# Dense weights built eight groups ahead instead of five, dense products from tile 15 instead of 22, and a reordered hand-over into the second sum of a fused graph kernel

## The reference

```
agg_l  = segment_sum((h @ W_l.T)[src] * norm, dst)          # 3 rounds
h      = elu(agg_l + b_l) + h
x1     = layernorm(x + concat(h0..h3) @ lin_w.T + lin_b)
W_r    = sum_b w_comp[r, b] * bases[b]                       # 8 relations, 4 bases
agg_r  = segment_sum(x1[src] * edge_weight, type * N + dst)
out    = layernorm(x1 + sum_r agg_r[r] @ W_r)
```

## Time and profile before

| | us |
|---|---|
| median of 3 runs | 1145.95 |
| lowest, highest | 1143.07, 1146.01 |
| the profiled execution | 1150.11 |
| its span in the trace | 1148.3 |
| from the first row of chunk 0 on PE to the end of the span | 579 |

### The profile page before, as it was taken

The page is one execution under the profiler, slowest core; times in us unless marked ns, Lnnn a source line. Parts: engine busy times, 40 slices in busy tenths (PEclk is TensorE's granted clock), DMA queues, the critical chain, the costliest instruction groups (busy, mean ns, idle before and its releaser), DMA issues.

```text
span 1148.3 us, 23479 instructions
## 1 busy us (share of the span) xinstructions
PE 1043.0 (91%) x9505; PEld 691.3 (60%) x9508; DVE 817.7 (71%) x1702; ACT 445.0 (39%) x1027; POOL 509.9 (44%) x542
## 2 busy tenths in 40 slices
PE   1678889889999999995489999999999999999997
PEld 1566556555644564465366666676666666666665
DVE  4689899887546556887566776876876776776753
ACT  1588889887300040025233332332332332332320
POOL 5043000000067400000377777776776766766761
PEclk9777899889999999997589999999999999999999
DMA  6163000000111010100422222222212212212210
GB/s 162 43 186 90 1 1 1 1 1 1 56 22 27 9 56 1 48 9 15 130 55 54 59 54 59 58 52 54 59 49 56 58 50 54 59 49 54 58 49 24
DMA packets 48801, 55.34 MB, mean 48 GB/s; under 512 B 15543, under 2 KB 39129, under 8 KB 48182
## 3 DMA queue, kind: packets, MB, share of 16 engines
q0 software_dynamic: 16240, 31.95, 11.2%
q1 hardware_dynamic: 32454, 21.87, 6.6%
HBM read 42.10 MB, written 8.49 MB: 44 GB/s over the span
## 4 chain that ended last, share of the span: by engine, by line
PE 72%; DVE 13%; issue 5%; SPq 3%; DMA 2%; POOL 2%; ACT 2%; DVEq 1%; ACTq 0%
PE ps L1679 21%; PE ps L1532 20%; PE ps L1658 15%; PE ps L1673 10%; DVE arena L1108 8%; PE ps L1521 2%; SPq L681 2%; POOL arena L838 2%; PE ps L1686 1%; PE ps L1692 1%; PE ps L1479 1%; SPq L738 1%; DMA dinv_col<-dinv_scratch 1%; DVE arena L1262 1%; PE ps L1509 1%
## 5 line engine op out<-in xcount | busy, mean ns | idle before, releaser
L838 POOL DMA_INDIRECT arena<-x_scratch,arena x437 | 412.9, 945 | 195.2 <-issue 124.2
L1532 PE MATMUL ps<-arena,u 125*128 125x480 fp8e5 (+1 forms) x1575 | 363.0, 357 | 1.2 <-ACT arena L892 1.2
L973 ACT COPY arena<-ps 125x400 f32<-125x400 f32 x364 | 169.6, 524 | 390.0 <-PE ps L1673 367.5
L1679 PE MATMUL ps<-arena,u 125*128 125x448 f32 x650 | 296.0, 539 | 0.0
L1658 PE MATMUL ps<-hT,arena 128*128 128x192 f32 x874 | 226.5, 352 | 13.1 <-DMA arena<-x_scratch,arena 13.0
L1532 PEld LDWEIGHTS ps<-arena,u 125*128 125x128 bf16 x1575 | 153.5, 98 | 107.9 <-ACT arena L892 1.7
L1658 PEld LDWEIGHTS ps<-hT,arena 128*128 128x128 f32 x874 | 148.8, 192 | 97.1 <-issue 67.7
L1108 DVE TENSOR_TENSOR arena<-arena 128x2048 bf16<-128x2048 bf16 (+2 forms) x158 | 188.9, 1253 | 18.5 <-PE ps L1521 15.5
L1521 PE MATMUL ps<-arena 128*128 128x125 bf16 x1256 | 151.9, 236 | 32.4 <-DVE arena L1108 30.7
L1673 PEld LDWEIGHTS ps<-dinv_all,u 64*128 64x128 bf16 x4368 | 108.4, 96 | 107.4 <-issue 92.2
L1323 DVE TENSOR_TENSOR u<-ps,arena 128x512 bf16<-128x512 bf16 x182 | 76.5, 420 | 122.7 <-PE ps L1673 114.0
(11 more groups left out here) (187 smaller groups left out, 717.1 us busy)
## 6 DMA issues: line engine op xcount, KB each, us to landing
arena<-x_scratch,arena POOLq DMA_INDIRECT x437
arena<-hT SPq DMA_DIRECT2D x2, 1562.5 KB, 7.1
edge_scratch<-arena SPq DMA_DIRECT2D x5, 403.0 KB, 5.5
arena<-in_x_dram SPq DMA_DIRECT2D x1, 1562.5 KB
dinv_all<-dinv_scratch SPq DMA_DIRECT2D x1, 1562.5 KB, 8.5
h_scratch<-hT SPq DMA_DIRECT2D x1, 1562.5 KB, 6.9
first_term_scratch<-arena SPq DMA_DIRECT2D x1, 1562.5 KB
arena<-first_term_scratch SPq DMA_DIRECT2D x1, 1562.5 KB
```

The costliest lines, as they stand in the source:

```text
L838: nc.gpsimd.indirect_dma_start(out=gat[:, j, :], out_offset=None, in_=x1_d, in_offset=bass.IndirectOffsetOnAxis(ap=idxg[:, j:j + 1], axis= ...
L973: nc.scalar.copy(o, ps[0:BLK, octet_bank(k, w), 0:4 * ND].rearrange("p (i m) -> p m i", i=4)).then_inc(s_se, 1)
L1532: return T.matmul(ps[:, agg_bank(l, c), 0:CW[c]], u[0:BLK, s, k, :], region[:, s, 0:CW[c]], start=(first and s == 0 and k == 0), stop=(end ...
L1679: last = T.matmul(ps[:, 5, 0:NB * DN].rearrange("p (b n) -> p b n", b=NB), xb[0:BLK, s, :], sD[half][0:BLK].rearrange("p (b v) n -> p b v ...
```

## The change

- `QA` goes from 5 to 8: three more octets in the prologue, three fewer in chunk 12.
- `DJ` goes from 22 to 15: a full chunk does 18 of its own products and 7 of the previous chunk's, in place of 11 and 14. `DLEFT` goes from 14 to 7.
- In chunk 12 the products stand one per tile from tile 15, not two per tile from 22; the last chunk of 8 tiles gets 7 of them in place of 3, and its `finish_dense` and `finish` move from tile 5 to tile 7.
- The two refills are bound to the octet's number in its own group (`prepare`): they now stand ahead of the octets after tile 14 and after tile 30 of a chunk, and one in the prologue; before, after tile 4 and after tile 21.
- SP no longer waits for `s_var` ahead of the x1 stores; the load of the basis matrices is issued behind them.
- DVE's third coefficient part is made after the loop over the seven groups, not before it.

```diff
-    QA = 5
-    DJ = 22
+    QA = 8
+    DJ = 15
@@ sync
-            sp.wait_ge(s_var, NUB)
-            sp.dma_start(basesS[:, :, :], bases.rearrange("b i o -> i b o")).then_inc(s_bas, 16)
             for j in range(NUB):
                 ...
                 sp.wait_ge(s_x1, j + 1)
                 sp.dma_start(x1_d[...], xb[0:BLK, b0:b1, :]).then_inc(s_x1d, 16)
+            sp.dma_start(basesS[:, :, :], bases.rearrange("b i o -> i b o")).then_inc(s_bas, 16)
@@ vector
-            dve.wait_ge(s_cq, 4)
-            V.tensor_tensor(coefP[:, :, 2 * NB:3 * NB, :], coefT, coefP[:, :, NB:2 * NB, :], ALU.subtract).then_inc(s_cp, 1)
             for t in range(NUB + 1):
                 ...
+            dve.wait_ge(s_cq, 4)
+            V.tensor_tensor(coefP[:, :, 2 * NB:3 * NB, :], coefT, coefP[:, :, NB:2 * NB, :], ALU.subtract).then_inc(s_cp, 1)
             dve.wait_ge(s_back[0], 32)
@@ vector, second sum
+                def prepare(c, k):
+                    h, m = c + k // QD, k % QD
+                    if m == HQ and h + 1 < DH:
+                        refill(h + 1, 0, False)
+                    if m == 0 and h >= 1:
+                        refill(h, 1, False)
...
-                                if k == HQ and following == TPB:
-                                    refill(c + 1, 0, False)
-                                if k == QD:
-                                    refill(c + 1, 1, False)
+                                prepare(c, k)
                                 octet(c, k)
...
                 for k in range(QA):
+                    prepare(0, k)
                     octet(0, k)
@@ tensor, second sum
                         if j >= DJ:
-                            for s in ((j - DJ,) if following else (2 * (j - DJ), 2 * (j - DJ) + 1)):
-                                dense(s, half)
+                            dense(j - DJ, half)
...
                 for j in range(LTILES):
                     tile(C, j, LTILES)
-                    if 2 * (TPB - DJ) + j < NBLK:
-                        dense(2 * (TPB - DJ) + j, 0)
-                    if j == 2 * BT - 1:
+                    if j < DLEFT:
+                        dense(TPB - DJ + j, 0)
+                    if j == LTILES - 1:
                         finish_dense(DH - 1, 6)
                         pe.wait_ge(s_af, C)
                         pe.wait_ge(s_dv, DH - 1)
```

## The result

The changed kernel takes 1129.24 us (median of 4, 1125.61 to 1131.82) against 1145.89 (median of 4): over all runs a ratio of 0.9859, interval 0.9832 to 0.9885. The forecast was 1130.0.

A forecast was written before the change was run, and what follows sets the result against it. PE's work bounds the full chunks; before chunk 0, PE waits on the chain of x1, stores, gather, tile 0. Terms -9.9 + 0.5 - 10.8 + 4.3 = -15.9 us from median 1145.95 give 1130.0 us, range 1124 to 1138.

The forecast's parts named there:

- Loop over the groups earlier: Hand-over on DVE: without L1253 ahead of it, the loop starts and x1 is complete 5.4 us earlier.
- DVE's gap: Ahead of L1282: the 2.44 us of flag reading and branch may vanish under L1253; taken as 0.1 us.
- Prologue: Before chunk 0: octets start 1.86 us apart, the ninth at 559.4, so tile 0 can start at 560.5.
- rival 3: Hand-over does not move: the last store's landing holds the first gather; only chunks 12 and 13 gain, 1139.5; chance 0.08.
- Stores: SP at the hand-over: some 2.3 us to issue each, keeping up with the groups; first gather by 545.5, 14.5 us earlier.
- Chunk 0: First chunk after the prologue: ends at 599.4 against 609.3, gain 9.9 us, with 2.5 us charged for cold PE.
- Chunks 1 to 11: Full chunks: DVE may stall PE in tiles 7 to 14, without products; 0 to 1.1 us in all, taken 0.5.
- Chunk 12 and the last chunk: End of the second sum: chunk 12 saves 10.8 us of products and octets; L1692 in the last chunk costs 4.3.
- Sum: Whole kernel: the terms add to -15.9 us, giving 1130.0 us from the median 1145.95.
- The clock: PE in the prologue: all nine octets charged at granted clock 0.50; a rise to 1.00 would save up to 4 us.
- rival 2: The prologue warms: octet activity raises PE's clock, shortening the prologue; 1123.5 to 1127 us; chance 0.12.

The follow-up runs named there:

- e4: Kernel before with only DVE reordered: third coefficient part behind the loop over the groups; 1140.8 us, ratio 0.996.
- e1: Kernel before with the reordered hand-over alone (x1 stores without s_var wait, basis load behind them, third coefficient part behind the loop), QA 5, DJ 22; 1130.3 us, ratio 0.9872.
- e6: Changed kernel with the refill of the second half ahead of octet 16 of a chunk instead of octet 14; 1126.2 us, ratio 0.9832.
- e5: Changed kernel with extra matmuls of zeros that keep PE busy before and between the prologue octets; 1127.0 us, ratio 0.9845.
- e2: Changed kernel with the old hand-over put back (basis load ahead of the stores, third coefficient part ahead of the loop), QA 8, DJ 15; 1143.0 us, ratio 0.9982.
- e8: Changed kernel with DJ back at 22 and the last chunk as before, QA 8 and the new hand-over kept; 1125.9 us, ratio 0.9832.
- e7: Changed kernel with both the extra zero matmuls on PE and the later refill of the second half; 1127.3 us, ratio 0.984.
- e3: Kernel before with only SP reordered: x1 stores without the wait for s_var, basis load behind them; 1132.7 us, ratio 0.9892.
- e11: Kernel before with the reordered hand-over (QA 5, DJ 22) plus extra zero matmuls on PE in the prologue; 1131.4 us, ratio 0.9852.
- e10: Changed kernel with extra zero matmuls, later refill and SP's three row reloads held for two batches of tiles, on a slower chip; 1309.4 us.
- e12: Changed kernel with extra zero matmuls, later refill and SP's three row reloads held, rerun on a chip of usual speed; 1128.2 us, ratio 0.9836.

## Why the prediction was right, and where it was not

- *Loop over the groups earlier*: forecast 5.4 us; measured 5.35 (the loop starts 5.38 us behind post before, 0.03 after), and e4 shows it as 5.2 at the end.
- *DVE's gap*: taken as 0.1, bounds 0 and 2.44. It is gone, and e4, e1 and the changed kernel all have the first octet at 27.8. L1281 starts without a gap behind L1271, so the flag is read while L1271 runs.
- *Prologue*: nine octets, 1.86 us apart, at half clock; tile 0 forecast at 44.0, measured at 44.23. The gathers are off the path there, as forecast; the first one is 15.05 us earlier, so rival 3 did not occur.
- *Stores*: right in place, wrong in one reading. The prediction takes 2.3 us as what a store costs SP; alone, one costs it 0.25. The forecast only needed the stores to keep up with the groups, which they do all the more, so the sum is untouched.
- *Chunk 0*: 37.83 us from tile 0 to the opening of chunk 1 against 38.9 forecast. A mean clock of 0.96 over 37.9 us is 3.0 us at half clock, which costs at most 1.5: the charge of 2.5 us for the cold start was about 1 us too high.
- *Chunks 1 to 11*: right place and mechanism, wrong size. The prediction took 0.5 us with a bound of 1.1; it is 1.8, of which e6 gives back 1.7. The wait also stands ahead of tile 15, not under the octet after tile 14.
- *Chunk 12 and the last chunk*: -6.5 forecast from the opening of chunk 12 to L1692; measured 44.67 against 51.38, -6.7. PE does not wait for a gather there.
- *Sum*: -15.9 forecast, -15.56 measured from post on. The charge too high in chunk 0 and the stall too low behind it nearly cancel. That the median lies within 0.8 us of 1130.0 is luck: the four runs are spread over 6 us.
- *The clock*: rival 2's mechanism exists (e5), but nine octets alone do not raise the clock: 0.50 throughout. The Trainium skill ("TensorE: Matmul & The Clock Gate", Part 1, What's actually happening) says that activity releases the throttle. The rows of e5 agree: from 540 to 552 PE is busy for 3.56 to 3.70 of each 4 us, and the granted clock is 1.00. In the kernel after, with the octets alone, PE is busy for 2.37 of 4 us, and the clock stayed at 0.50.
- *Rival 3* priced the table at 6.5 us without the hand-over. e2 gives 3.5: of the difference 1.7 is the stall in chunks 1 to 11 and 1.1 chunk 0.

What the prediction had wrong is a sentence that the number survived: "work taken from chunk 12 and put into chunk 0 or before it, where PE has room, is worth its full PE time". For the three octets it holds, near enough (2.5 us of 2.6, e1 to e8), since chunk 0 still had gathers to wait for even behind the new hand-over. For the seven products it does not: once the octets stand ahead, chunk 0 has almost no room left, and they cost 4.2 us there for 4.1 saved at the end, with the stall on top. The sum came out since each stretch was walked through in order and not priced as a separate gain. Had the parts of the change been priced apart, it would have shown that the hand-over gives 15.2 of 15.6 us by itself.

No version tried is faster than the changed kernel beyond the scatter of the times. By the profiles e5 is shortest from post to the end (612.8 against 616.3), then e7, e8 and e6.

## What to carry to other kernels

Two edits that fill the same idle time do not add. Walk the path once with both in place, and again with each alone, before crediting either; and where an edit has two parts, take it apart too, since a gain of 2.5 us and a loss of 2.1 look like one edit that does nothing. What work costs where it is moved to is read at the next place where something else was late: the three octets put tile 0 5.6 us later and chunk 1 only 0.3 us later. And where executions scatter more than the edit is worth, count from a mark behind the part that is unchanged: 9 of the 24.6 us between these two traces had nothing to do with the change.

## What the runs showed of the hardware beyond that

- Reading a flag and branching on DVE cost 2.44 us behind short instructions in the kernel before, 1.23 us in e3, also behind short ones, and nothing behind a running one of 3.35 us. What sets it between 1.23 and 2.44, no run shows.
- PE stood still inside a run of matmuls without any wait, for 3.00 us (e7) and 3.27 us (e11). In both, the 28th 16 KB packet of the instruction queue started only after PE had stopped, with 7361 and 7357 matmuls and weight loads started; in the ten profiles without such a gap, from chips of the usual speed, it started at 7108 to 7230. That PE ran out of instructions fits; no edit tests it.
- The same program (e10 and e12) took 1309 us on one chip and 1128 us on another. PE was busy for 53 us more, and from 640 us on it waited 75.8 us for ACT's evictions of octets, up to 4.6 us at a time, where on the other chip it never did.
- A 250 KB store of 512-byte rows took SP 0.25 to 0.27 us to issue when it came 1.7 to 3.2 us behind the one before, and 2.0 to 2.4 us in a block of seven, with a DMA share of 0.37. What SP waits for in a block, the profile does not show.
